# Low parts of tokens and two of four countings on GpSimd, and wider VectorE instructions in the rotation and the counting of an attention and FFN phase

## The chip, the cores and the metric

The kernel runs on one core of a Trainium2 chip. The core has TensorE (PE in the profile; PEld is its weight load), VectorE (DVE), ScalarE (ACT), GpSimd (POOL) and SyncE (SP, which here issues DMAs). The engines run their own instruction streams in order and wait for each other by semaphores. The metric is the device time in microseconds, the median of several runs.

## The reference

Four sequences of 1024 tokens with 256 features pass through two layers. Layer 0 is a gated convolution block with an MLP, and then a mixture of 32 experts. Layer 1 is block-masked attention with rotary positions (16 heads of 16), and then a gated FFN with a 2:4 choice: of every four neighbouring hidden values the two largest in magnitude are kept. What the change touches is in layer 1:

```python
def _rope(x):
    ...
    x1, x2 = jnp.split(x, 2, axis=-1)
    rot = jnp.concatenate([-x2, x1], axis=-1)
    return x * cos + rot * sin
...
def _sparsify_2to4(h):
    g = h.reshape(B, S, I // 4, 4)
    a = jnp.abs(g)
    _, idx = jax.lax.top_k(a, 2)
    pos = jnp.arange(4)
    mask = (pos == idx[..., 0:1]) | (pos == idx[..., 1:2])
    return (g * mask.astype(g.dtype)).reshape(B, S, I)
...
h = jax.nn.silu(jnp.einsum('bsh,hi->bsi', x, w_gate)) * jnp.einsum('bsh,hi->bsi', x, w_up)
h_sparse = _sparsify_2to4(h)
return jnp.einsum('bsi,ih->bsh', h_sparse, w_down)
```

## The kernel before, in words

Three phases run one after the other: `conv_mlp_phase` (layer 0's first half), `experts_phase`, and `attention_ffn_phase` (layer 1), which takes the time from 678 us on. The change lies in the third alone. All tokens stay in `x_sb`, 32 tiles of 128 tokens; a sequence has 8 tiles (`ST`), treated in two halves of 4 (`GT`).

For each sequence `b` the third phase normalises the tokens, projects them to q, k and v, rotates q and k, takes for every head and row of blocks the maximum of the scores, computes the scores again with that maximum subtracted, their exponentials and the weighted sums (`heads`), projects out, normalises, and runs the FFN. FFN of sequence `b` and projections of sequence `c = b + 1` are woven together. I call this stretch a joint; there are three, since the last sequence has nothing after it. In the first it lies at 880 to 1012 us.

The order of each engine is written out by hand, in one function per engine: `@block.sync`, `@block.gpsimd`, `@block.scalar`, `@block.vector`, `@block.tensor`. Within a joint the FFN goes in 16 passes `w`. A pass of PE (`hidden`, L2067) makes 128 hidden features in 24 matmuls, then ACT takes SiLU (`silu`, L1540), DVE multiplies gate and up (`hidden`, L1722: one input in PSUM, one in SBUF; below it is the product of pass `w`), and ACT takes the magnitude (`magnitude`, L1546). PE may be two passes ahead of DVE's product: `hidden(b, w)` on PE waits for `hm_ok` of pass `w - 2`.

The projections of sequence `c` use f16 pairs: a tile is rounded to f16 by ACT (`x_high`, L1478), and what is left is the low part (`x_low`, L1638, on DVE, 256 columns). SP turns both by a transposing DMA (`x_turned`, L1379), which waits for the low part; PE multiplies (`qkv`, L1910) into one bank, ACT copies q and k out of it, then v (`qkv_copied`, L1485, L1488). DVE rotates (`rotate`): q and k times cosine (L1646), times sine (L1649), and two additions (L1652, L1653). ACT makes the high parts and copies (`high_part`, L1495; `part_copies`), DVE the low parts of q and k (`low_parts`, L1658, L1659). In pass `w` DVE does `rotate(c, w + 1)`, the product, `low_parts(c, w + 1)` and `x_low(c, w + 4)`.

The 2:4 choice works on groups of four passes, `k` = 0 to 3: `compare` (L1732 to L1734) compares the magnitudes pairwise into six planes `ge` of bf16, `count` (L1739 to L1747) adds and subtracts these planes to four counts `nb`, and `keep_largest` (L1756, the keep) multiplies the values by whether their count suffices. Three steps share the semaphore `sp`. In a joint, `compare(b, 0)` follows pass 4, `count(b, 0)` pass 5, the keep pass 6; `compare(b, 1)` and `count(b, 1)` follow pass 8, and the second keep comes after two maxima of sequence `c` (L1669) and the product of pass 9. `sparsify(b, 2)` and `sparsify(b, 3)` do the three steps at a stretch. PE's `down` (L2080) needs the kept values.

POOL in this phase computes only the inverse deviations of the layer norms (`inverse_deviation`, L1440 and L1443, on 4 columns) in the order of the list `ORDER`, and sets some columns by memset (`zero_columns`, L1447). The normalisation itself (`normal`, L1622) is DVE's and waits for `rs_ok`.

In the first phase POOL adds and multiplies whole tiles (L234, L239, L247) while DVE convolves (L396, two inputs in SBUF).

Of the kernel before, what the change touches and what calls it, by code (L numbers as in the profile page):

```python
# [22 lines left out]
P = 128  # L23
# [1134 lines left out]
def attention_ffn_phase(nc, io, keep):  # L1158
    with ExitStack() as ctx:  # L1159
# [9 lines left out]
        w_fd = sb("w_fd", [P, NF, D])  # L1169
        cos = sb("cos", [P, ST, HD])  # L1170
        sin = sb("sin", [P, ST, HD])
        mask = sb("mask", [P, 2])
# [5 lines left out]
        qk = sb("qk", [P, 2, 2 * HEADS, HD])  # L1178
        ro = sb("ro", [P, 2 * HEADS, HD])
        sn = sb("sn", [P, 2 * HEADS, HD])  # L1180
        xbT = sb("xbT", [P, KD, SEQ])
# [183 lines left out]
        def _(sync):  # L1365
            for src in ("w_qk", "w_v"):
                sync.dma_start(raw[src].rearrange("p (k c) -> p k c", k=KD), io[src]).then_inc(w_loaded, 16)
            for src, dst in (("mask", mask), ("cos", cos), ("sin", sin)):
                sync.dma_start(dst[:], io[src]).then_inc(consts, 16)
            for src in ("w_fg", "w_fu"):  # L1370
                sync.dma_start(raw[src].rearrange("p (k c) -> p k c", k=KD), io[src]).then_inc(wf_loaded, 16)
            for src, dst in (("w_o", w_o), ("w_fd", w_fd)):
                sync.dma_start(dst[:], io[src]).then_inc(consts, 16)

# [61 lines left out]
        def _(pool):  # L1436
            def inverse_deviation(k):
# [5 lines left out]
                pool.tensor_tensor(rs[:], ve[:], power[:], ALU.pow).then_inc(rs_ok, 1)  # L1443

            def zero_columns(c):
                all_q_max_landed(pool, c)
                pool.memset(all_rows[:, 0, :, NORM:FILTER], 0.0).then_inc(zeroed, 1)  # L1447
# [13 lines left out]
            for k in range(2, len(ORDER)):  # L1461
                kind, b, s = ORDER[k]
                inverse_deviation(k)
                if (kind, s) == ("a", 0) and b + 1 < NB:
                    zero_columns(b + 1)

        @block.scalar
        def _(act):
# [11 lines left out]
            def qkv_copied(c, t):  # L1480
                k = c * ST + t
                wait(act, qkv_mm, k + 1)
                wait(act, turned, 2 * (k - 1))
                bank = tile_bank(c, t)
                act.activation(qk[:, t % 2, :, :].rearrange("p h d -> p (h d)"), bank[:, 0, :], ACT.Copy, scale=1 / W_SCALE)  # L1485
                if t == 0 and c > 0:
                    wait(act, pv_mm, LEAD + c * NHG * NU)
                act.activation(v[:, t, :, 0:HD], bank[:, 1, 0:D].rearrange("p (h d) -> p h d", h=HEADS),  # L1488
                               ACT.Copy, scale=1 / W_SCALE).then_inc(qkv_ok, 1)
# [112 lines left out]
        def _(dve):  # L1602
# [37 lines left out]
            def rotate(c, t):  # L1640
# [4 lines left out]
                wait(dve, low_ok, k)  # L1645
                dve.tensor_tensor(ro[:, :, :], x, cos[:, t, :].unsqueeze(1).to_broadcast([P, 2 * HEADS, HD]),  # L1646
                                  ALU.mult).then_inc(turned, 1)
                wait(dve, rv_ok, k)
                dve.tensor_tensor(sn[:, :, :], x, sin[:, t, :].unsqueeze(1).to_broadcast([P, 2 * HEADS, HD]),  # L1649
                                  ALU.mult).then_inc(turned, 1)  # L1650
                wait(dve, turned, 2 * k + 2)
                dve.tensor_tensor(ro[:, :, 0:HALF_D], ro[:, :, 0:HALF_D], sn[:, :, HALF_D:], ALU.add)  # L1652
# [83 lines left out]
            def count(b, k):  # L1736
                s = 3 * (4 * b + k)
                wait(dve, sp, s + 1)
                dve.tensor_tensor(nb[:, 0, :], ge[:, 0, :], ge[:, 1, :], ALU.add)  # L1739
                dve.tensor_tensor(nb[:, 1, :], ge[:, 3, :], ge[:, 4, :], ALU.add)  # L1740
                dve.tensor_tensor(nb[:, 2, :], ge[:, 1, :], ge[:, 3, :], ALU.add)
                dve.tensor_tensor(nb[:, 3, :], ge[:, 2, :], ge[:, 4, :], ALU.add).then_inc(sp, 1)
                wait(dve, sp, s + 2)
                dve.tensor_tensor(nb[:, 0, :], nb[:, 0, :], ge[:, 2, :], ALU.add)
                dve.tensor_tensor(nb[:, 1, :], nb[:, 1, :], ge[:, 0, :], ALU.subtract)
                dve.tensor_tensor(nb[:, 2, :], nb[:, 2, :], ge[:, 5, :], ALU.subtract)
                dve.tensor_tensor(nb[:, 3, :], nb[:, 3, :], ge[:, 5, :], ALU.add).then_inc(sp, 1)  # L1747

# [31 lines left out]
            def heads(b):  # L1780
                for g in range(NHG):
                    for s in range(STEPS):
# [7 lines left out]
                        if g == NHG - 1:  # L1790
                            if b > 0 and s in (2, 6):
                                finish(b - 1, s // 4)
                            if b + 1 < NB and s in (10, 14):
                                layernorm("x", b + 1, s // 4 - 2)
                if b + 1 < NB:
                    x_low(b + 1, 0)
                    x_low(b + 1, 1)
                normalised(b, NHG - 1, 1)
# [25 lines left out]
            for b in range(NB):  # L1824
# [11 lines left out]
                if ahead:  # L1836
                    x_low(c, 2)
                    rotate(c, 0)
# [4 lines left out]
                normal("a", b, 1)  # L1843
                if ahead:
                    x_low(c, 3)
                for w in range(NF + 1 if ahead else 16):
# [5 lines left out]
                    if ahead and w + 1 < ST:  # L1852
                        low_parts(c, w + 1)
                    if ahead and w + 4 < ST:
                        x_low(c, w + 4)
                    if w >= 4 and w % 4 == 0:
                        compare(b, w // 4 - 1)
                    if w >= 4 and w % 4 == 1 or ahead and w == NF:
                        count(b, w // 4 - 1)
# [369 lines left out]
```

## Time and profile before

| | |
|---|---|
| runs | 1753.49, 1753.75 and 1754.46 us, median 1753.75 |
| profiled execution | 1749.66 us, its span 1747.8 us |
| mean granted clock of TensorE | 0.917 |
| PE busy | 1479.3 us (85%) |
| DVE busy | 1146.7 us (66%) |
| ACT busy | 732.6 us (42%) |
| POOL busy | 219.9 us (13%) |

The profile is of one execution. Busy time of an engine is the time in which at least one of its instructions ran; PE overlaps matmuls, so a busy PE is not a PE at its peak. Two instructions in a row on DVE overlap a little: one of 512 columns lasts 0.68 us and the next starts 0.60 us after it. Such a distance from start to start is what an instruction costs in a row. POOL's 220 us lie almost all in the first two phases.

### The profile page before, as it was taken

To read this page: it belongs to the slowest core of one execution; us is meant where nothing else is said; L and a number is where in the kernel's file an instruction comes from. 1 tells how busy PE (TensorE), PEld (TensorE's weight loads), DVE (VectorE), ACT (ScalarE), POOL (GpSimd) and SP (SyncE) were. 2 spreads that over 40 slices of the span, in tenths; PEclk is the share of its full clock that TensorE was granted. 3 is DMA by queue.
4 is the path that set the end of the run, shared out by engine and by line. 5 is a ranking of instruction groups with operands and counts; after the bars stand their busy time and mean duration, and the time that the engine had idled before them with its cause. 6 is when DMAs were issued, how large, how long until landed. Compare 5 with 4: busy or idle time off the path is not lost.

```text
span 1747.8 us, 25797 instructions
## 1 busy us (share of the span) xinstructions
PE 1479.3 (85%) x9682; PEld 826.3 (47%) x9683; DVE 1146.7 (66%) x2395; ACT 732.6 (42%) x1232; POOL 219.9 (13%) x225
## 2 busy tenths in 40 slices
PE   4999999967989983588878998887998788988796
PEld 2566666653657773223343533253533344433354
DVE  5566666636421135678668769668789578789475
ACT  5454444512212220426744137743147652157530
POOL 3344444411410001000000000100000100000000
PEclk8999999978999987759998979998989898989999
DMA  2000000005105412212101023111013111211000
GB/s 111 13 25 25 24 24 24 28 21 180 40 26 150 149 39 105 47 33 43 31 19 31 1 43 56 40 19 28 17 28 60 38 19 24 37 37 32 31 1 25
DMA packets 137483, 75.21 MB, mean 43 GB/s; under 512 B 117648, under 2 KB 126352, under 8 KB 136592
## 3 DMA queue, kind: packets, MB, share of 16 engines
q1 hardware_dynamic: 136800, 72.02, 16.8%
q0 software_dynamic: 576, 1.77, 0.4%
q8 instruction: 67, 1.10, 0.3%
q14 instruction: 40, 0.33, 0.1%
HBM read 37.59 MB, written 9.06 MB: 27 GB/s over the span
## 4 chain that ended last, share of the span: by engine, by line
issue 59%; POOL 2%; DVE 0%; POOLq 0%; DVEq 0%
POOL rs_sb L1443 1%; POOL ve_sb L1440 0%; POOL qks_sb L1457 0%; POOL v_sb L1455 0%; DVE bn_sb L1607 0%; DVE x_sb_sb L1622 0%; POOLq L1159 0%; POOLq L66 0%; POOL qks_sb L1447 0%; DVE mv_sb L1613 0%; DVEq L1159 0%; POOL v_sb L1454 0%; POOL qks_sb L1458 0%; DVE ident_h_sb L1803 0%; DVEq L66 0%
## 5 line engine op out<-in xcount | busy, mean ns | idle before, releaser
L1509 ACT ACTIVATE room_sb<-s_ps 128x1024 f32<-128x1024 f32 (+1 forms) x320 | 291.2, 941 | 167.1 <-PE s_ps L1965 162.5
L1674 DVE TENSOR_REDUCE mx_sb<-s_ps 128x1 f32<-128x512 f32 (+1 forms) x400 | 249.4, 649 | 63.5 <-PE s_ps L1941 40.2
L1938 PE MATMUL s_ps<-room_sb 48*128 48x512 f16 (+3 forms) x480 | 152.3, 354 | 30.6 <-DVE mx_sb L1669 16.3
L1985 PE MATMUL cm_ps<-room_sb,v_sb 128*32 128x512 f32 (+3 forms) x1536 | 166.2, 522 | 0.8 <-ACT room_sb L1515 0.8
L1965 PE MATMUL s_ps<-room_sb 51*128 51x128 f16 (+4 forms) x1152 | 150.4, 283 | 15.4 <-ACT room_sb L1509 10.6
L2080 PE MATMUL cm_ps<-w_fd_sb,room_sb 128*128 128x256 f32 x512 | 131.6, 405 | 14.6 <-DVE room_sb L1756 14.6
L1440 POOL TENSOR_TENSOR ve_sb<-mv_sb,eps_sb 128x4 f32<-128x4 f32 x24 | 5.0, 210 | 1027.9 <-DVE mv_sb L1613 1027.9
L396 DVE SCALAR_TENSOR_TENSOR x_sb_sb<-xp_sb,conv_w_sb,x_sb_sb 128x512 f32<-128x512 f32 x96 | 106.9, 1117 | 22.6 <-ACT x_sb_sb L319 20.5
L2067 PE MATMUL s_ps<-xbT_sb,w_fg_sb 128*128 128x512 f16 x384 | 107.3, 412 | 14.3 <-DVE ctok_sb L1722 12.7
L1938 PEld LDWEIGHTS s_ps<-room_sb 48*128 48x128 f16 x480 | 42.5, 95 | 161.7 <-DVE mx_sb L1674 85.0
L2080 PEld LDWEIGHTS cm_ps<-w_fd_sb,room_sb 128*128 128x128 f32 x512 | 97.2, 198 | 38.7 <-issue 14.3
L2067 PE MATMUL s_ps<-xbT_sb,w_fu_sb 128*128 128x512 f16 x384 | 102.9, 399 | 0.0
L966 PE MATMUL em_ps<-xT_sb,ws_gu_sb 128*128 128x512 f32 x192 | 92.1, 626 | 8.0 <-DMA rows<-zeros 8.0
L1910 PE MATMUL s_ps<-w_qk_sb,xt_sb 128*128 128x512 f16 x192 | 51.3, 406 | 49.2 <-DMA xt_sb<-xs_sb 31.4
L1965 PEld LDWEIGHTS s_ps<-room_sb 50*128 50x128 f16 (+1 forms) x1152 | 58.5, 97 | 65.8 <-ACT room_sb L1509 44.9
L1941 PE MATMUL s_ps<-room_sb 51*128 51x128 f16 x360 | 69.7, 238 | 19.6 <-DMA room_sb<-qks_sb 12.0
L1674 DVE TENSOR_REDUCE mx_sb<-cm_ps 128x1 f32<-128x512 f32 (+1 forms) x112 | 73.3, 655 | 18.2 <-PE s_ps L1941 13.9
L402 DVE SCALAR_TENSOR_TENSOR m1T_sb<-mm_ps,m1T_sb 128x512 f16<-128x512 f32 x64 | 44.0, 688 | 57.1 <-ACT m1T_sb L311 56.9
L1540 ACT ACTIVATE sgl_sb<-s_ps 128x512 f32<-128x512 f32 x64 | 37.9, 593 | 82.9 <-PE s_ps L2067 82.5
L490 PE MATMUL ro_ps<-w_dn_sb,m1T_sb 128*128 128x256 f16 x256 | 69.8, 273 | 0.8
L491 PE MATMUL ro_ps<-w_dn_sb,m1T_sb 128*128 128x256 f16 x256 | 69.8, 273 | 0.0
L492 PE MATMUL ro_ps<-w_dn_sb,m1T_sb 128*128 128x256 f16 x256 | 69.8, 273 | 0.0
(260 smaller groups left out, 2932.5 us busy)
## 6 DMA issues: line engine op xcount, KB each, us to landing
we_gu_sb<-we_gu SPq DMA_DIRECT2D x32, 352.0 KB
we_dn_sb<-we_dn SPq DMA_DIRECT2D x32, 176.0 KB
x_in_sb<-x SPq DMA_DIRECT2D x9, 512.0 KB, 3.6
rows<-x_sb_sb SPq DMA_DIRECT2D x8, 512.0 KB, 3.0
x_sb_sb<-rows SPq DMA_DIRECT2D x2, 2048.0 KB, 11.4
out<-x_sb_sb SPq DMA_DIRECT2D x8, 512.0 KB, 2.6
room_sb<-qks_sb SPq DMA_TRANSPOSE x88, 3.3
xp_sb<-w_in SPq DMA_DIRECT2D x1, 1024.0 KB, 5.4
```

The source lines that it names most:

```text
L396: dve.scalar_tensor_tensor(xc[:, c, :], xp[:, c, k:k + GTOK], conv_w[:, c, k:k + 1], xc[:, c, :], ALU.mult, ALU.add)\
L490: pe.matmul(out, of[0][at], by[0][cols], start=start, stop=False)
L491: pe.matmul(out, of[1][at], by[0][cols], start=False, stop=False)
L492: return pe.matmul(out, of[0][at], by[1][cols], start=False, stop=stop)
L966: last = pe.matmul(mm[c % 4][:, :], ws_gu[:, k, col:col + P], xT[:, k, g * GTOK:(g + 1) * GTOK], start=(k == 0), stop=(k == KD - 1))
L1509: act.activation(weights[(g * NU + u) % SLOTS_P][:, 2 * pair:2 * pair + 2, 0:width(u) * P], W[s % 2][:, :, 0:width(u) * P], ACT.Exp, scale ...
L1674: dve.tensor_reduce(mx[:, pair, k % 2, slot:slot + 1], max_bank(g, m)[:, 0:count * P], AX.X, ALU.max, negate=True).then_inc(mx_ok, 1)
L1938: last = pe.matmul(bank[:, at * P:(at + plain) * P], query[head:head + NORM, i * P:(i + 1) * P], key[head:head + NORM, j * P:(j + plain) * ...
L1965: last = pe.matmul(W[s % 2][:, head, (at + low - i) * P:(at + high - i) * P], key[first:first + rows, j * P:(j + 1) * P], query[first:firs ...
L1985: last = pe.matmul(O[32 * h:32 * h + 32, (i - half * GT) * P:(i - half * GT + count) * P], v[:, j, g * HG + h, :], weights[(g * NU + u) % ...
L2067: last = pe.matmul(bank[:, e, :], wt[:, j, k, ch * P:(ch + 1) * P], xh[:, g, k, i, :], start=(k == n == 0), stop=(k == KD - 1 and n == 2))
L2080: last = pe.matmul(CM[:, t // 2, (t % 2) * D:(t % 2 + 1) * D], hs[:, k % 3 * 4 + i, t * P:(t + 1) * P], w_fd[:, k % 2 * 4 + i, :], start=( ...
```

## The change

1. `x_low` of the second, third and fourth sequence goes from DVE to POOL (24 instructions; those of the first sequence stay). POOL has them in its list behind the inverse deviations: tiles 0 and 1 behind that of `("x", b, 1)`, tile 2 behind `("a", b, 0)` and ahead of the memset, tiles 3 to 7 behind `("a", b, 1)`.
2. In the three joints `count(b, 0)` and `count(b, 1)` go to POOL, behind tile 7's low part.
3. Counting takes four instructions of two planes each (1024 columns) for eight of one plane, on either engine.
4. `ro` and `sn` become planes of one tile `rosn`, `cos` and `sin` of `tables`, and the two multiplications of a rotation become one instruction of 1024 columns. It has both waits in front, and `turned` counts one step a tile instead of two.

```diff
-        cos = sb("cos", [P, ST, HD])
-        sin = sb("sin", [P, ST, HD])
+        tables = sb("tables", [P, 2, ST, HD])
...
-        ro = sb("ro", [P, 2 * HEADS, HD])
-        sn = sb("sn", [P, 2 * HEADS, HD])
+        rosn = sb("rosn", [P, 2, 2 * HEADS, HD])
+        ro, sn = rosn[:, 0, :, :], rosn[:, 1, :, :]
...
         @block.gpsimd
...
+            def x_low(c, t):
+                k = c * ST + t
+                wait(pool, xs_high, k + 1)
+                xt_landed(pool, k - 2)
+                pool.tensor_tensor(xs[:, t % 2, 1, :], x_tile(c, t), xs[:, t % 2, 0, :], ALU.subtract).then_inc(xs_low, 1)
+
+            def count(b, k):
+                s = 3 * (4 * b + k)
+                wait(pool, sp, s + 1)
+                wait(pool, hs_ok, 4 * b + k)
+                pool.tensor_tensor(nb[:, 0:2, :], ge[:, 0:4:3, :], ge[:, 1:5:3, :], ALU.add)
+                pool.tensor_tensor(nb[:, 2:4, :], ge[:, 1:3, :], ge[:, 3:5, :], ALU.add).then_inc(sp, 1)
+                wait(pool, sp, s + 2)
+                pool.tensor_tensor(nb[:, 0:4:3, :], nb[:, 0:4:3, :], ge[:, 2:6:3, :], ALU.add)
+                pool.tensor_tensor(nb[:, 1:3, :], nb[:, 1:3, :], ge[:, 0:6:5, :], ALU.subtract).then_inc(sp, 1)
...
                 inverse_deviation(k)
-                if (kind, s) == ("a", 0) and b + 1 < NB:
-                    zero_columns(b + 1)
+                if (kind, s) == ("x", 1):
+                    x_low(b, 0)
+                    x_low(b, 1)
+                if kind == "a" and b + 1 < NB:
+                    x_low(b + 1, 2 + s)
+                    if s == 0:
+                        zero_columns(b + 1)
+                    else:
+                        for t in range(4, ST):
+                            x_low(b + 1, t)
+                        for n in range(2):
+                            count(b, n)
...
         @block.vector
...
-                dve.tensor_tensor(ro[:, :, :], x, cos[:, t, :].unsqueeze(1).to_broadcast([P, 2 * HEADS, HD]),
+                wait(dve, rv_ok, k)
+                dve.tensor_tensor(rosn[:, :, :, :], x.unsqueeze(1).to_broadcast([P, 2, 2 * HEADS, HD]),
+                                  tables[:, :, t, :].unsqueeze(2).to_broadcast([P, 2, 2 * HEADS, HD]),
                                   ALU.mult).then_inc(turned, 1)
-                wait(dve, rv_ok, k)
-                dve.tensor_tensor(sn[:, :, :], x, sin[:, t, :].unsqueeze(1).to_broadcast([P, 2 * HEADS, HD]),
-                                  ALU.mult).then_inc(turned, 1)
-                wait(dve, turned, 2 * k + 2)
+                wait(dve, turned, k + 1)
...
-                dve.tensor_tensor(nb[:, 0, :], ge[:, 0, :], ge[:, 1, :], ALU.add)
-                dve.tensor_tensor(nb[:, 1, :], ge[:, 3, :], ge[:, 4, :], ALU.add)
-                dve.tensor_tensor(nb[:, 2, :], ge[:, 1, :], ge[:, 3, :], ALU.add)
-                dve.tensor_tensor(nb[:, 3, :], ge[:, 2, :], ge[:, 4, :], ALU.add).then_inc(sp, 1)
+                dve.tensor_tensor(nb[:, 0:2, :], ge[:, 0:4:3, :], ge[:, 1:5:3, :], ALU.add)
+                dve.tensor_tensor(nb[:, 2:4, :], ge[:, 1:3, :], ge[:, 3:5, :], ALU.add).then_inc(sp, 1)
...
-                if ahead:
-                    x_low(c, 2)
                     rotate(c, 0)
...
-                    if ahead and w + 4 < ST:
-                        x_low(c, w + 4)
...
-                    if w >= 4 and w % 4 == 1 or ahead and w == NF:
+                    if not ahead and w >= 4 and w % 4 == 1:
                         count(b, w // 4 - 1)
```

How the order of the engines changes is shown at two places. The first is POOL in the first joint, from the inverse deviation of the first half of the attention's output on (`xs_sb` holds the f16 pairs, `room_sb` the planes `ge`, `nb_sb` the counts). Before:

```order
L1440 TENSOR_TENSOR ve_sb<-mv_sb,eps_sb 128x4
L1443 TENSOR_TENSOR rs_sb<-ve_sb,power_sb 128x4
L1447 MEMSET qks_sb 128x128x2
L1440 TENSOR_TENSOR ve_sb<-mv_sb,eps_sb 128x4
L1443 TENSOR_TENSOR rs_sb<-ve_sb,power_sb 128x4
```

Now:

```order
L1442 TENSOR_TENSOR rs_sb<-ve_sb,power_sb 128x4
L1448 TENSOR_TENSOR xs_sb<-x_sb_sb,xs_sb 128x256
L1462 MEMSET qks_sb 128x128x2
L1439 TENSOR_TENSOR ve_sb<-mv_sb,eps_sb 128x4
L1442 TENSOR_TENSOR rs_sb<-ve_sb,power_sb 128x4
L1448 TENSOR_TENSOR xs_sb<-x_sb_sb,xs_sb 128x256 x5
L1454 TENSOR_TENSOR nb_sb<-room_sb 128x1024
L1455 TENSOR_TENSOR nb_sb<-room_sb 128x1024
L1457 TENSOR_TENSOR nb_sb<-nb_sb,room_sb 128x2x512
L1458 TENSOR_TENSOR nb_sb<-nb_sb,room_sb 128x1024
```

A low part now stands between the first inverse deviation and the memset, five more behind the second, and then the counts, of which the first is shown; the second follows at once.

The second place is DVE from the second comparison of a joint to the keep behind it. Before:

```order
L1734 TENSOR_TENSOR room_sb<-room_sb 128x512
L1739 TENSOR_TENSOR nb_sb<-room_sb 128x512
L1740 TENSOR_TENSOR nb_sb<-room_sb 128x512
L1741 TENSOR_TENSOR nb_sb<-room_sb 128x512
L1742 TENSOR_TENSOR nb_sb<-room_sb 128x512
L1744 TENSOR_TENSOR nb_sb<-nb_sb,room_sb 128x512
L1745 TENSOR_TENSOR nb_sb<-nb_sb,room_sb 128x512
L1746 TENSOR_TENSOR nb_sb<-nb_sb,room_sb 128x512
L1747 TENSOR_TENSOR nb_sb<-nb_sb,room_sb 128x512
L1669 TENSOR_REDUCE mx_sb<-s_ps 128x2 x2
L1722 SCALAR_TENSOR_TENSOR room_sb<-s_ps,sgl_sb 128x512
L1756 SCALAR_TENSOR_TENSOR room_sb<-nb_sb,ctok_sb 128x512 x4
```

Now:

```order
L1758 TENSOR_TENSOR room_sb<-room_sb 128x512
L1693 TENSOR_REDUCE mx_sb<-s_ps 128x2 x2
L1746 SCALAR_TENSOR_TENSOR room_sb<-s_ps,sgl_sb 128x512
L1776 SCALAR_TENSOR_TENSOR room_sb<-nb_sb,ctok_sb 128x512 x4
L1693 TENSOR_REDUCE mx_sb<-s_ps 128x2 x2
```

The eight counting instructions are gone from between the comparison and the maxima; the keep, two maxima and one product later, waits for POOL's count, and two more maxima stand behind it.

## Rows read from the trace of the kernel before

**Rows 1.** The page, part 1: busy time of each engine (share of the span).

```profile
PE 1479.3 (85%) x9682; PEld 826.3 (47%) x9683; DVE 1146.7 (66%) x2395; ACT 732.6 (42%) x1232; POOL 219.9 (13%) x225
```

**Rows 2.** Waits of PE, 880 to 1012 us: total, times, longest.

```profile
PE s_ps L2067 <- DVE ctok_sb L1722: 4.2, 2, 3.6
...
PE cm_ps L2080 <- DVE room_sb L1756: 3.3, 1, 3.3
...
PE s_ps L1938 <- DVE mx_sb L1669: 2.5, 1, 2.5
```

**Rows 3.** Timeline of DVE, first joint: start, us, instruction [idle before <-releaser].

```profile
908.84 0.42 DVE L1638 TENSOR_TENSOR xs_sb<-x_sb_sb,xs_sb 128x256 f16<-128x256 f32 x1 [1.43 <-ACT xs_sb L1478]
...
914.14 0.42 DVE L1638 TENSOR_TENSOR xs_sb<-x_sb_sb,xs_sb 128x256 f16<-128x256 f32 x1 [1.43 <-ACT xs_sb L1478]
...
932.03 0.68 DVE L1734 TENSOR_TENSOR room_sb<-room_sb 128x512 bf16<-128x512 f32 x1
...
932.63 0.68 DVE L1646 TENSOR_TENSOR ro_sb<-qk_sb,cos_sb 128x512 f32<-128x512 f32 x1
...
936.09 0.42 DVE L1739 TENSOR_TENSOR nb_sb<-room_sb 128x512 bf16<-128x512 bf16 x1
...
938.90 0.68 DVE L1646 TENSOR_TENSOR ro_sb<-qk_sb,cos_sb 128x512 f32<-128x512 f32 x1
...
940.89 0.68 DVE L1722 SCALAR_TENSOR_TENSOR ctok_sb<-s_ps,sgl_sb 128x512 f32<-128x512 f32 x1
```

**Rows 4.** Timeline of PE, same joint.

```profile
936.68 1.46 PE L2067 MATMUL s_ps<-xbT_sb,w_fu_sb 128*128 128x512 f16 x6
...
941.72 2.72 PE L2067 MATMUL s_ps<-xbT_sb,w_fg_sb 128*128 128x512 f16 x6 [3.58 <-DVE ctok_sb L1722]
...
959.02 0.39 PE L1938 MATMUL s_ps<-room_sb 48*128 48x256 f16 x1
...
963.31 12.79 PE L2080 MATMUL cm_ps<-w_fd_sb,room_sb 128*128 128x256 f32 x58
```

**Rows 5.** Timeline of DVE, around the second comparison and keep.

```profile
951.08 0.68 DVE L1734 TENSOR_TENSOR room_sb<-room_sb 128x512 bf16<-128x512 f32 x1
...
955.87 2.49 DVE L1756 SCALAR_TENSOR_TENSOR room_sb<-nb_sb,ctok_sb 128x512 f32<-128x512 bf16 x4
```

**Rows 6.** Groups of POOL by line: count | busy us, mean ns | idle before.

```profile
L247 POOL TENSOR_TENSOR yT_sb<-x_sb_sb,yT_sb 128x512 f16<-128x512 f32 x32 | 35.9, 1153 | 0.0
...
L731 POOL TENSOR_TENSOR su_sb<-sg_sb,su_sb 128x512 f32<-128x512 f32 x9 | 11.4, 1262 | 47.3 <-ACT su_sb L767 47.3
...
L736 POOL TENSOR_TENSOR x_sb_sb<-x_sb_sb,so_sb 128x1024 f32<-128x1024 f32 x8 | 18.8, 2351 | 137.7 <-ACT so_sb L773 137.7
```

**Rows 7.** L396 (ns min/median/max), then timelines of DVE and POOL, first phase.

```profile
L396 DVE SCALAR_TENSOR_TENSOR x_sb_sb<-xp_sb,conv_w_sb,x_sb_sb x96: 734/752/2760, 19.7 to 325.5; 128x512 f32<-128x512 f32 x96
...
98.23 2.75 DVE L396 SCALAR_TENSOR_TENSOR x_sb_sb<-xp_sb,conv_w_sb,x_sb_sb 128x512 f32<-128x512 f32 x1
...
97.88 2.56 POOL L234 TENSOR_TENSOR x_sb_sb<-x_in_sb,x_sb_sb 128x1024 f32<-128x1024 f32 x1
...
102.94 1.68 POOL L239 TENSOR_TENSOR x_sb_sb<-x_sb_sb 128x512 f32<-128x512 f32 x1 [2.50 <-ACT x_sb_sb L296]
```

**Rows 8.** Timelines of DVE and POOL, start of the third phase.

```profile
686.53 5.72 DVE L1622 TENSOR_SCALAR x_sb_sb<-x_sb_sb,mv_sb,rs_sb 128x256 f32<-128x256 f32 x3 [1.49 <-POOL rs_sb L1443]
...
688.22 2.91 POOL L1457 MEMSET qks_sb<- 128x1664 f16 x2
```

**Rows 9.** Group of DVE by line, 1024 f32.

```profile
L1773 DVE TENSOR_TENSOR x_sb_sb<-cm_ps,x_sb_sb 128x1024 f32<-128x1024 f32 x8 | 9.7, 1217 | 2.5 <-PE cm_ps L2080 2.5
```

**Rows 10.** Timeline of ACT, same joint.

```profile
913.43 0.37 ACT L1488 ACTIVATE v_sb<-s_ps 128x256 f32<-128x256 f32 x1
```

**Rows 11.** DMA issues, 895 to 935 us: count, median us to landing.

```profile
xt_sb<-xs_sb SPq DMA_TRANSPOSE x6, 2.5
```

**Rows 12.** Stretches: us, busy of PE, PEld, DVE, ACT, POOL, PEclk, DMA, GB/s.

```profile
955.00:961.20 6.20, 6.11 (x21) 1.78 (x21) 5.11 (x10) 1.23 (x2) 0.00 (x0) 0.50 0.00 0
```

More of the change, by code:

```diff
@@ L1367, in _ @@
                 sync.dma_start(raw[src].rearrange("p (k c) -> p k c", k=KD), io[src]).then_inc(w_loaded, 16)
-            for src, dst in (("mask", mask), ("cos", cos), ("sin", sin)):
-                sync.dma_start(dst[:], io[src]).then_inc(consts, 16)
+            for src, dst in (("mask", mask), ("cos", tables[:, 0, :, :]), ("sin", tables[:, 1, :, :])):
+                sync.dma_start(dst if src in ("cos", "sin") else dst[:], io[src]).then_inc(consts, 16)
             for src in ("w_fg", "w_fu"):
@@ L1372, in _ @@
             for src, dst in (("w_o", w_o), ("w_fd", w_fd)):
-                sync.dma_start(dst[:], io[src]).then_inc(consts, 16)
+                sync.dma_start(dst if src in ("cos", "sin") else dst[:], io[src]).then_inc(consts, 16)
             def x_turned(c, t):
@@ L1482, in qkv_copied @@
                 wait(act, qkv_mm, k + 1)
-                wait(act, turned, 2 * (k - 1))
+                wait(act, turned, k - 1)
                 bank = tile_bank(c, t)
@@ L1738, in count @@
                 wait(dve, sp, s + 1)
-                dve.tensor_tensor(nb[:, 0, :], ge[:, 0, :], ge[:, 1, :], ALU.add)
-                dve.tensor_tensor(nb[:, 1, :], ge[:, 3, :], ge[:, 4, :], ALU.add)
-                dve.tensor_tensor(nb[:, 2, :], ge[:, 1, :], ge[:, 3, :], ALU.add)
-                dve.tensor_tensor(nb[:, 3, :], ge[:, 2, :], ge[:, 4, :], ALU.add).then_inc(sp, 1)
+                dve.tensor_tensor(nb[:, 0:2, :], ge[:, 0:4:3, :], ge[:, 1:5:3, :], ALU.add)
+                dve.tensor_tensor(nb[:, 2:4, :], ge[:, 1:3, :], ge[:, 3:5, :], ALU.add).then_inc(sp, 1)
                 wait(dve, sp, s + 2)
[L1744 to L1747, printed above, removed]
+                dve.tensor_tensor(nb[:, 0:4:3, :], nb[:, 0:4:3, :], ge[:, 2:6:3, :], ALU.add)
+                dve.tensor_tensor(nb[:, 1:3, :], nb[:, 1:3, :], ge[:, 0:6:5, :], ALU.subtract).then_inc(sp, 1)
             def keep_largest(b, k):
@@ L1794, in heads @@
                                 layernorm("x", b + 1, s // 4 - 2)
-                if b + 1 < NB:
-                    x_low(b + 1, 0)
-                    x_low(b + 1, 1)
                 normalised(b, NHG - 1, 1)
@@ L1843, in _ @@
                 normal("a", b, 1)
-                if ahead:
-                    x_low(c, 3)
                 for w in range(NF + 1 if ahead else 16):
```

## The prediction

> **What bounds the kernel now.** I read the busy times first: TensorE (PE) works 85% of the span, VectorE (DVE) 66%, GpSimd (POOL) 13% [rows 1]. PE's waits in the first joint (880 to 1012 us, where the FFN of one sequence meets the projections of the next) come next: 4.2 us for the gated products L1722, 2.5 us for a maximum, 3.3 us for kept values L1756 [rows 2]. All three are DVE's. There are three such joints (sequences 0 to 1, 1 to 2, 2 to 3), and only there does the change move work to POOL. DVE's timeline shows why it is late: after the first comparison ends, at 932.63, it still has to rotate, count and rotate again before the product of pass 6 at 940.89, for which PE sat idle 3.58 us [rows 3, 4]. After the second comparison it counts until the keep at 955.87, and PE stalls again [rows 4, 5]. So DVE's order sets the end here; work that leaves DVE is worth something only if nothing in that order then waits for POOL.
>
> **What POOL charges.** A two-input instruction of 512 f32 takes 1.262 us there and of 1024 f32 2.351, so 2.13 ns an element and 0.17 fixed; with f16 in one input and the output, 512 take 1.153 [rows 6]. A counting instruction has 1024 elements, all bf16, a form that no row has. From above the 1024 f32 row bounds it: 2.35. From below I let 16 bits halve the element part, as they do on DVE (0.42 for 512 bf16 against 0.68 in f32 [rows 3]): 1.26. I take twice 1.153 less one fixed part, 2.13, since the f16 row is the nearest. A count is 4 of these, 8.6 us with its inner wait (4.9 to 9.5), against 2.8 us on DVE (936.09 to 938.90) [rows 3]. A low part (256) is half the 512 f16 row less the fixed part's share: about 0.6.
> The page GPSIMD Engine Reference of the Trainium skill (3.1, side-by-side cycle accounting) gives 4497 ns for 2048 f32 elements; 1024 would be an estimated 2.25 us, a count 9.0, and the predicted time 3 us higher (0.12 for each of 8 instructions in 3 joints). The row of 1024 f32 here is 4% above that figure; the page says nothing of 16 bits, and the f16 row is 9% under its f32 fellow.
>
> **What POOL does to DVE.** This decides the case. In the first phase a DVE instruction with both inputs in SBUF (L396, median 0.752 us) that starts beside a 2.56 us POOL instruction lasts 2.75 and ends 0.54 after it; the other way round a POOL instruction of 512 f32, 1.262 alone, becomes 1.68 while DVE finishes [rows 6, 7]. So they take turns, whole instructions at a time. The normalisation L1622 is worse off: three of them, 768 elements and so less work than the 1.217 us of 1024, need 5.72 us beside a row of memsets on POOL, and do not get in between these [rows 8, 9]. In the joint, rotations, low parts of q and k, and keeps all have two SBUF inputs. Maxima and gated products read PSUM and at most one tile of SBUF.
> SBUF — State Buffer of the Trainium skill (Who interferes with whom) makes this a rule against the change: a DVE instruction with two SBUF inputs contends with a POOL instruction that reads SBUF. The rows show it for f32; for bf16 no run here does yet.
>
> **The change part by part**, for one joint, against the trace.
> (a) Low parts. Off DVE they save 0.34 each (0.42 less what overlaps), plus the wait for ScalarE: period of a pass 908.84 to 914.14 is 5.30, of which 1.43 waits [rows 3]. The next rotation then starts when q and k are copied (913.43 and 0.37 [rows 10]) instead of 0.68 later. But POOL's low part becomes ready 0.3 after that, during the multiplication, and goes before the additions, which wait 0.55 to 0.6: DVE gives back most of it. With the fused multiplication (next) a pass gains 0.3; four passes, -1.2. The other four stand in POOL's queue in front of or among normalisations: two before the normalisation of x (+0.3, since 0.7 of their DVE time also goes), one with the memset before that of the first half (+0.8 - 0.34), one before the second (+0.6 - 0.34). Each low part also releases the transposing DMA of its tile; it now ends some 1.7 us into a pass, and 2.5 us later [rows 11] the tile has landed, still before the 5.0 at which PE's next projection finds its bank free: no cost. What else stands behind POOL's new work, the inverse deviations, is asked for only 8 us or more later.
> (b) Fused rotation. Two multiplications of 512 are issued 0.60 apart; an instruction of 1024 f32 lasts 1.217 [rows 9] and lets the next start some 0.08 sooner, 1.13. That is -0.07 a rotation, -0.14 for the two outside the passes. (a) and (b): -1.2 + 0.3 + 0.46 + 0.26 - 0.14 = -0.3. The bounds are -3.4 (no turns lost) and +1.
> (c) First count. Let C be the end of the first comparison. Before: product of pass 6 ends at C+8.9, second comparison ends C+19.05 (951.08 + 0.60) [rows 3, 5]. After: multiplication to C+1.15, then in turns POOL 2.0 (a queued one is issued early), addition 0.3, POOL 2.0, addition, product 5 beside POOL's third, low part, POOL's fourth to C+10.1. Then low part, rotation 7 (2.0) and product 6 end at C+12.9, keep C+13.7 to 16.1, product 7 C+16.8. PE starts its pass 8 at C+12.95 rather than C+9.1 and needs twice 1.46 less their overlap, 2.6 us, or 5.2 at the lower clock [rows 4]; the second comparison ends at C+20.8 or C+22.7. I take the middle: +2.7. With the low price it is +0.3, with the high one +3.6.
> (d) Second count. Nothing contends here, but the keep waits for all of it: from the comparison's end, E, it began at E+4.2 (955.87 - 951.68) [rows 5]; now at E+0.1+8.4 = E+8.5, +4.3. Queued behind it on DVE are the maxima that PE needs for 959.02 [rows 4], so PE moves by the same. Two maxima and a product in front of it run earlier, which helps nobody past it. PE then idles some 8 us. After the 2.5 us idle for a maximum the granted clock was 0.50 (1.2 GHz) [rows 2, 12], and after the 3.58 us six matmuls took 2.72 us instead of 1.46 [rows 4]; so the rest of pass 11 (4.29 us [rows 4], half of it at full clock) goes slowly: +1.2 (-0.8 to +2). Together +5.5; low price +1.2, high +7.
> (e) The other counts stay on DVE: 4 instructions of 0.34 + 0.27 instead of 8 of 0.34 is 2.4 for 2.7, -0.3. The third is hidden behind PE's down products (from 963.31 [rows 4]); the fourth is what L2080 waits for [rows 2], so -0.3 per joint.
> Sum: -0.3 + 2.7 + 5.5 - 0.3 = +7.6 a joint, +22.8 for three. The last sequence has its counts on DVE, -0.9 for the three that are not hidden, and the first rotations give -0.3: **+21.6**. The profiled execution (span 1747.8 in 1749.66) becomes 1771.3; the median of the runs is 1753.75, 4.1 above it, so the predicted time is 1775.
>
> **The rivals.** First, DVE isn't held by 16-bit counts and half-f16 low parts: place, the two rotations after C. For it: no row shows such a pair. Against it: every f32 pair of the first phase takes turns. Then (a) and (b) give -3.4 and (c) gives -1.0 at 2.13 but -2.8 once a count is under 6.5 us; (d) stays. At the middle price that is -3.4 - 1.0 + 5.5 - 0.3 = +0.8, or 1755; at 1.26 it is -5.3 a joint, 17 in all: 1737. It turns faster below some 2.0 us an instruction.
> Second, turns are taken but bf16 runs at the low price: -0.3 + 0.3 + 1.2 - 0.3 = +0.9 a joint, less 1.2: 1755, hardly to be told from no change.
> Third, the high price, PE slow for all of pass 8 and pass 11 and no gain from (a): +1 + 5.5 + 7 - 0.3 = +13 a joint, 1792. For it speaks that PE's longest idle here, 3.58 us, already halved the clock, and that (d) makes one of 8.
>
> **How the numbers follow.** Forecast 0.62 (1775); not held 0.08; cheap bf16 0.12; dear and slow 0.18. A run of this kernel can be told from no change at 0.2%, 3.5 us. Faster by more than that needs the first rival at a low price: 0.08. Within it lies most of the second: 0.10. Slower: 0.82. The range 1755 to 1794 leaves out the first rival, half of the second and little of the third. Its ends are the bounds of the counting instruction's price.
>
> **What would show it.** In the new profile: POOL's counting instructions at 2.0 to 2.2 us; the rotation right after the first comparison drawn out over some 9 us; the second keep about 8.5 us behind its comparison with DVE idle for POOL; a wait of PE for a maximum of some 8 us, followed by a 0.50 clock; POOL's low parts beside lengthened additions. I am wrong if the counting rows are near 1.2 us, if rotations beside them keep their usual durations, or if PE's total wait in a joint shrinks.

## The result, and the profile after

The changed kernel takes 1779.6 us (median of four runs, 1779.17 to 1781.71) against 1753.62 for the kernel before beside it: 1.0156 times as long, 95% interval 1.0136 to 1.0176. 1775 was predicted, in a range of 1755 to 1794, so the slowdown is 26 us for 21.6. The profiled execution has a span of 1777.8 us at a mean granted clock of 0.907.

The first line of the page answers to [rows 1]: VectorE's busy time hardly moves, GpSimd gains 80 us, and TensorE is busy 10 us longer with the same matmuls.

```profile
PE 1489.0 (84%) x9682; PEld 834.3 (47%) x9683; DVE 1145.8 (64%) x2251; ACT 733.4 (41%) x1232; POOL 299.7 (17%) x273
```

TensorE's waits in the first joint (880 to 1022 us; total, times, longest) answer to [rows 2]:

```profile
PE s_ps L1950 <- DVE mx_sb L1693: 9.1, 1, 9.1
PE s_ps L2079 <- DVE ctok_sb L1746: 6.6, 2, 4.2
...
PE cm_ps L2092 <- DVE room_sb L1776: 3.1, 1, 3.1
```

The wait for a maximum (2.5 before) is 9.1 us and the one for products (4.2) is 6.6. VectorE's timeline of that joint (L1672 is the fused multiplication, L1676 and L1677 the additions, L1746 the product, L1682 and L1683 the low parts of q and k, L1758 the end of a comparison, L1776 the keep):

```profile
909.99 1.23 DVE L1672 TENSOR_TENSOR rosn_sb<-qk_sb,tables_sb 128x1024 f32<-128x1024 f32 x1 [1.12 <-ACT v_sb L1513]
911.25 0.78 DVE L1676 TENSOR_TENSOR rosn_sb<-rosn_sb 128x256 f32<-128x256 f32 x1
...
914.94 1.23 DVE L1672 TENSOR_TENSOR rosn_sb<-qk_sb,tables_sb 128x1024 f32<-128x1024 f32 x1 [1.13 <-ACT v_sb L1513]
...
932.68 1.22 DVE L1672 TENSOR_TENSOR rosn_sb<-qk_sb,tables_sb 128x1024 f32<-128x1024 f32 x1
933.93 2.22 DVE L1676 TENSOR_TENSOR rosn_sb<-rosn_sb 128x256 f32<-128x256 f32 x1
936.08 2.33 DVE L1677 TENSOR_TENSOR rosn_sb<-rosn_sb 128x256 f32<-128x256 f32 x1
938.33 0.68 DVE L1746 SCALAR_TENSOR_TENSOR ctok_sb<-s_ps,sgl_sb 128x512 f32<-128x512 f32 x1
939.10 1.57 DVE L1682 TENSOR_TENSOR qks_sb<-rosn_sb,qks_sb 128x256 f16<-128x256 f32 x1
940.60 2.34 DVE L1683 TENSOR_TENSOR qks_sb<-rosn_sb,qks_sb 128x256 f16<-128x256 f32 x1
...
945.08 0.68 DVE L1746 SCALAR_TENSOR_TENSOR ctok_sb<-s_ps,sgl_sb 128x512 f32<-128x512 f32 x1
...
946.53 2.49 DVE L1776 SCALAR_TENSOR_TENSOR room_sb<-nb_sb,room_sb 128x512 f32<-128x512 bf16 x4
...
954.42 0.68 DVE L1758 TENSOR_TENSOR room_sb<-room_sb 128x512 bf16<-128x512 f32 x1
...
963.68 2.50 DVE L1776 SCALAR_TENSOR_TENSOR room_sb<-nb_sb,ctok_sb 128x512 f32<-128x512 bf16 x4 [7.31 <-POOL nb_sb L1458]
```

GpSimd's timeline, the two counts (first and last instruction of each; beside the first one the durations include turns with VectorE):

```profile
932.84 3.03 POOL L1454 TENSOR_TENSOR nb_sb<-room_sb 128x1024 bf16<-128x1024 bf16 x1 [5.56 <-DVE room_sb L1758]
...
940.35 2.31 POOL L1458 TENSOR_TENSOR nb_sb<-nb_sb,room_sb 128x1024 bf16<-128x1024 bf16 x1
955.18 2.13 POOL L1454 TENSOR_TENSOR nb_sb<-room_sb 128x1024 bf16<-128x1024 bf16 x1 [12.52 <-DVE room_sb L1758]
...
961.53 2.11 POOL L1458 TENSOR_TENSOR nb_sb<-nb_sb,room_sb 128x1024 bf16<-128x1024 bf16 x1
```

Beside the first count the two additions and the two low parts, 0.42 us each otherwise, take 2.22, 2.33, 1.57 and 2.34: 6.8 us more together, while the product between them keeps its 0.68. The same four are drawn out in the other two joints, to within 0.01 us. The count's result is not late: it ends at 942.66, and the first keep comes only at 946.53. Nothing is stretched beside the second count, but the keep stands idle for it. TensorE's timeline, and below it the stretches (us, busy times, PEclk the granted clock):

```profile
939.06 2.39 PE L2079 MATMUL s_ps<-xbT_sb,w_fg_sb 128*128 128x512 f16 x6 [4.19 <-DVE ctok_sb L1746]
...
945.91 2.38 PE L2079 MATMUL s_ps<-xbT_sb,w_fg_sb 128*128 128x512 f16 x6 [2.39 <-DVE ctok_sb L1746]
948.08 2.27 PE L2079 MATMUL s_ps<-xbT_sb,w_fu_sb 128*128 128x512 f16 x6
950.18 1.46 PE L2079 MATMUL s_ps<-xbT_sb,w_fg_sb 128*128 128x512 f16 x6
...
966.83 0.39 PE L1950 MATMUL s_ps<-room_sb 48*128 48x256 f16 x1 [9.10 <-DVE mx_sb L1693]
```

```profile
966.80:972.70 5.90, 5.87 (x17) 1.37 (x17) 2.84 (x5) 0.92 (x2) 0.00 (x0) 0.50 0.00 0
972.70:987.50 14.80, 14.80 (x60) 12.45 (x58) 9.73 (x13) 0.94 (x2) 0.00 (x0) 0.85 0.01 2
...
1147.00:1156.30 9.30, 8.09 (x30) 6.80 (x29) 1.23 (x1) 1.33 (x2) 0.00 (x0) 0.60 0.02 4
```

After the 9.1 us of idling the rest of pass 11 runs wholly at 1.2 GHz (0.50), and the first 60 down matmuls need 14.8 us at 0.85. In the other two joints pass 11 is slow as well, but the down matmuls run at 1.00 and 0.99. (The last line belongs to the entry of the second joint, below.)

Where the time goes, from one mark of the two profiles to the next (after less before, us):

| stretch of a joint | predicted | first | second | third |
|---|---|---|---|---|
| attention residual (L1788) to C, end of the first comparison | -0.3 | -1.1 | -1.4 | -1.4 |
| C to E, end of the second comparison | +2.7 | +3.3 | +5.5 | +3.1 |
| E to the second keep | +4.3 | +4.5 | +4.5 | +4.5 |
| second keep to the first residual (L1793) | +1.2 | +3.7 | +0.4 | +1.7 |
| first to second residual | -0.3 | -1.3 | -1.5 | +1.3 |
| second residual to the next joint's L1788 | 0 | +2.8 | +2.2 | -1.0 |

That is 25.7 inside the joints and 4.0 between them, with 1.2 ahead of the first joint and -1.0 in the last sequence: 30 us between the two profiled executions, where the medians differ by 26. The 4.0 are of one pair of executions, and the one of before was 4.1 us under its own median. The low parts need not be behind them. With none of them on GpSimd the last stretch of the table takes 122.3 us behind the first joint in one run below (fused rotation and two planes alone) and 122.3 behind the second in another (low parts back on VectorE); it is 119.3 and 120.1 before, 122.1 and 122.3 now. At the entry of the second joint the order is the same in both but for the low parts, and TensorE's output projection had a clock of 0.79 before (next line) and 0.60 after (last line above):

```profile
1135.00:1143.30 8.30, 7.08 (x33) 6.29 (x34) 1.23 (x1) 1.33 (x2) 0.00 (x0) 0.79 0.16 32
```

### The profile page after: what moved, and what is told of

It reads as the page before. It is cut to its first block and busy times, and to the rows that moved or that the text cites. A ratio compares the mean times of both kernels' runs of the same rounds, so it can differ in the third digit from the quotient of the medians.

```text
span 1777.8 us, 25737 instructions
## 1 busy us (share of the span) xinstructions
PE 1489.0 (84%) x9682; PEld 834.3 (47%) x9683; DVE 1145.8 (64%) x2251; ACT 733.4 (41%) x1232; POOL 299.7 (17%) x273
## 5 line engine op out<-in xcount | busy, mean ns | idle before, releaser
L2079 PE MATMUL s_ps<-xbT_sb,w_fg_sb 128*128 128x512 f16 x384 | 108.8, 417 | 20.8 <-DVE ctok_sb L1746 19.4
L396 DVE SCALAR_TENSOR_TENSOR x_sb_sb<-xp_sb,conv_w_sb,x_sb_sb 128x512 f32<-128x512 f32 x96 | 106.8, 1115 | 22.6 <-ACT x_sb_sb L319 20.5
```

What stands on the lines that cost most here:

```text
L396: dve.scalar_tensor_tensor(xc[:, c, :], xp[:, c, k:k + GTOK], conv_w[:, c, k:k + 1], xc[:, c, :], ALU.mult, ALU.add)\
L2079: last = pe.matmul(bank[:, e, :], wt[:, j, k, ch * P:(ch + 1) * P], xh[:, g, k, i, :], start=(k == n == 0), stop=(k == KD - 1 and n == 2))
```

## The experiments

My theory: the second count costs by its latency, since the keep waits for it with maxima queued behind, and by the clock after that; the first costs by turns with two-input instructions on VectorE; the other parts gain a little. The first four kernels take the change apart.

**Both counts back on VectorE**

```diff
-                        for n in range(2):
-                            count(b, n)
...
-                    if not ahead and w >= 4 and w % 4 == 1:
+                    if w >= 4 and w % 4 == 1 or ahead and w == NF:
                         count(b, w // 4 - 1)
```

> Edit: the changed kernel with the first and second count of every joint back on VectorE (in two planes); low parts of tokens stay on GpSimd, the fused rotation stays. Theory (the second count makes the keep wait for GpSimd and TensorE drops its clock; the first count takes turns with rotations; the other parts gain a little): the first count cost about 10 to 12 us (the end of the second comparison moved by 3.3, 5.5 and 3.1 us in the three joints), the second about 19 (three times 4.5 and some 6 of clock), so 1748.5 us, 1745 to 1752, a little below the kernel before at 1753.6. Rival A (the low parts on GpSimd, in front of normalisations and beside rotations, are what costs): it stays above 1765. Rival B (the fused rotation or the two-plane counts are slower than what they replace): above 1756.

Measured: 1746.3 us, 0.9958 of before (0.9940 to 0.9975), as the theory has it; rivals A and B fall. The rest of the change is a small gain, and the counts on GpSimd cost more than the whole slowdown, 33 us by the medians. TensorE still waits for maxima behind the count and the keep (first joint):

```profile
PE s_ps L1948 <- DVE mx_sb L1691: 4.0, 2, 2.6
```

**Only the first count, and only the second, on GpSimd**

```diff
-                        for n in range(2):
-                            count(b, n)
+                        count(b, 0)
```

(and `count(b, 1)` in the other; VectorE does the one that is left.)

> Edit: the changed kernel with the second count of every joint back on VectorE; only the first one is on GpSimd. Theory (second count costs more than the first): 1748.5 and the 10 to 12 us of the first count, 1759 us, 1755 to 1763; GpSimd's counting instructions and the rotation beside them still end one after the other, the second keep no longer waits. Rival C (the turns are the main cost, the wait of the keep is covered by other work): 1770 to 1777. Rival A (the low parts cost): above 1770 as well, but then also without any count on GpSimd.

> Edit: the changed kernel with the first count of every joint back on VectorE; only the second one is on GpSimd. Theory: 1748.5 and the 19 us of the second count, 1767 us, 1762 to 1772; the second keep begins about 8.6 us behind its comparison and TensorE waits some 8 us for a maximum. Rival C (turns are the main cost): 1750 to 1757.

Measured: 1760.0 us (1.0034, 1.0017 to 1.0050) and 1761.3 us (1.0039, 1.0023 to 1.0054). So the first count costs 13.8 us and the second 15.1 over the kernel without them. Between the marks, against that kernel, the first keep comes 4.55 later in the joint with the first count on GpSimd, and the second keep 4.7 later with the second: three times each is 13.7 and 14.2. The second by itself is just under the range given. Each moved count costs about the same, where the theory had 10 to 12 us for the first and 19 for the second; rival C falls too. Both together, the changed kernel, are 0.0198 of 1754 or 35 us over the kernel with neither: some 6 more than the sum, which is about what the intervals leave open. In the profiles the part of it that can be seen is the clock: from the second keep to the first residual the kernel with both takes 2.6, 0.4 and 0.6 us longer than the one with the second count alone, and in the first joint TensorE's first 60 down matmuls behind that keep take 12.7 us at full clock with the second count alone, and 14.8 at 0.85 with both.

**Low parts of tokens back on VectorE**

```diff
-                    x_low(b + 1, 2 + s)
...
-                        for t in range(4, ST):
-                            x_low(b + 1, t)
...
+                    if ahead and w + 4 < ST:
+                        x_low(c, w + 4)
```

> Edit: the changed kernel with all low parts of tokens back on VectorE where they were; both counts stay on GpSimd. Theory (the low parts on GpSimd gain 1.1 to 1.4 us a joint, of which up to 0.3 is the fused rotation): 3 to 4 us slower than the changed kernel's 1779.6, 1783 us, 1780 to 1786. Rival A (the low parts cost): 1760 to 1772. Rival D (they neither gain nor cost): within 1 us of 1779.6.

Measured: 1781.3 us, 1.0156 of before (1.0143 to 1.0169), the same ratio as the changed kernel, so rival D by the ratios, although the median itself lies in the theory's range: the run does not decide between them. The profile does show the gain in the passes: a period of 5.24 here against 4.95 in the changed kernel (909.99 to 914.94 above), with the wait for ScalarE's high part (1.43) back in place of that for its copy (1.13 there):

```profile
913.01 0.43 DVE L1657 TENSOR_TENSOR xs_sb<-x_sb_sb,xs_sb 128x256 f16<-128x256 f32 x1 [1.43 <-ACT xs_sb L1497]
...
918.25 0.43 DVE L1657 TENSOR_TENSOR xs_sb<-x_sb_sb,xs_sb 128x256 f16<-128x256 f32 x1 [1.43 <-ACT xs_sb L1497]
```

From the attention residual to C the move gains 1.06, 1.04 and 0.96 us in the three joints (44.96 against 43.90 in the first). Together that is 3.1 us, less than the intervals are wide.

**Fused rotation and two planes alone**

The edit joins the two before: no count and no low part on GpSimd.

> Edit: the kernel with only the fused rotation and the counts in two planes; low parts of tokens and all counts are on VectorE, GpSimd gets nothing new. With counts on VectorE and low parts on GpSimd the time was 1746.3 us. Theory (as measured on the changed kernel, moving the low parts changes the time by no more than 1.5 us): 1747 us, 1745 to 1749.5, so the gain over the kernel before comes from the fused rotation and the two planes. Rival (the low parts on GpSimd gain once no count stands behind them): 1750 to 1754.

Measured: 1747.4 us, 0.9968 (0.9954 to 0.9981). These two edits make the gain, 5.6 us. What the low parts add (0.9958 against 0.9968) stays inside the intervals, so their worth to the whole kernel is not settled.

**The keep moved behind the maxima**

If the second count costs by what is queued behind its keep, one moved line must give it back.

```diff
                         hidden(b, w - 1)
-                        if w == 10:
-                            keep_largest(b, 1)
                         maxima(c, 0, m + 2, m + 4)
                     hidden(b, 11)
+                    keep_largest(b, 1)
                     sparsify(b, 2)
```

> Edit: the changed kernel with one line moved: the second keep of a joint stands after the maxima and the products of passes 10 and 11, right before the third comparison; the count that it needs is still on GpSimd. Theory (the second count costs by what is queued behind the waiting keep, and by the clock after it): the 4.7 us a joint and the clock behind it go, and the 2.6 and 1.3 us that TensorE waits for a maximum behind count and keep go too: 1760 us with the first count's price left, less up to 12: 1750 us, 1746 to 1762; TensorE's wait of some 9 us for a maximum is under 1 us. Rival E (what GpSimd does during that time slows VectorE's maxima and products as well, or the keep's wait moves on to the down products): 1768 to 1780.

Measured: 1742.4 us, 0.9930 (0.9909 to 0.9952): 37 us less than the changed kernel, with both counts still on GpSimd, and 3.6 below the range. TensorE's waits of the first joint have no row for a maximum any more. The price of the second count is gone and more with it. Against the kernel with the first count alone, the end of the second comparison to the first residual takes 6.5, 5.9 and 6.1 us less, and I had allowed for the 3.9 of the two waits. The rest is the clock: pass 11 and the down products now run at full clock (stretches of this run; compare 0.50 and 0.85 above), while with the first count alone the end of pass 11 had 0.50 in the first joint:

```profile
957.90:963.90 6.00, 6.00 (x35) 1.96 (x33) 4.82 (x10) 2.50 (x5) 5.75 (x3) 1.00 0.00 0
963.90:976.60 12.70, 12.70 (x60) 10.93 (x58) 10.96 (x16) 1.06 (x2) 2.65 (x2) 1.00 0.01 2
```

**The same with the first count on VectorE, and with all counts there**

```diff
-                        for n in range(2):
-                            count(b, n)
+                        count(b, 1)
```

(the keep late as above; in the second kernel neither count is on GpSimd, and `count(b, 1)` stands ahead of the late keep on VectorE.)

> Edit: as the run before it (second keep late), and the first count back on VectorE; second count on GpSimd. Theory: 1746.3 us of both counts on VectorE, less the waits of TensorE for a maximum behind the second count and keep (2.6 and 1.3 us a joint): 1736 us, 1733 to 1743; GpSimd's counting instructions 2.1 us each, since maxima and products read PSUM. Rival E: 1750 to 1765.

> Edit: no count on GpSimd; on VectorE the second count and the second keep both stand late, right before the third comparison. Theory (the place in VectorE's order decides, not the engine that counts): the maxima come as early as with the count on GpSimd, and the later count and keep of 4.9 us are still done before the second half of the down products needs them: 1736 us, 1733 to 1744, within 2 us of the run with the count on GpSimd. Rival F (it pays only because GpSimd does the counting, the late count delays the down products): 1744 to 1752.

Measured: 1729.5 us, 0.9866 (0.9846 to 0.9885), for the first, which beats both kernels, by 24 and by 50 us, and lies 3.5 us below the range. Again it is the clock that I had left out: in the first joint the kernel with both counts on VectorE ran the end of pass 11 at 0.50 and this one at 1.00. Its VectorE and GpSimd beside each other in the first joint:

```profile
950.21 0.69 DVE L1692 TENSOR_REDUCE mx_sb<-s_ps 128x2 f32<-128x512 f32 x1
...
957.62 2.50 DVE L1775 SCALAR_TENSOR_TENSOR room_sb<-nb_sb,ctok_sb 128x512 f32<-128x512 bf16 x4 [1.31 <-POOL nb_sb L1458]
```

```profile
949.11 2.12 POOL L1454 TENSOR_TENSOR nb_sb<-room_sb 128x1024 bf16<-128x1024 bf16 x1 [23.20 <-DVE room_sb L1757]
...
955.46 2.13 POOL L1458 TENSOR_TENSOR nb_sb<-nb_sb,room_sb 128x1024 bf16<-128x1024 bf16 x1
```

Maxima and products, which read PSUM, keep their durations beside the count (0.69 and 0.68), and the count keeps its 2.12.

With all counts on VectorE it is 1738.9 us, 0.9922 (0.9897 to 0.9947): by the ratios the place in VectorE's order alone gives 6 of the 16 us (0.0036 and 0.0092 of 1754) that lie between both counts on VectorE and the second one on GpSimd with a late keep. Rival F falls, but that the engine wouldn't matter was wrong: 1738.9 is 9 us above the run with the count on GpSimd, not within 2. The count ahead of the late keep puts the third comparison 1.2 us later, TensorE then waits 1.1 us for a maximum at the end of the first down products, and in the second and third joint its clock falls. These stretches of the second joint, of the run with all counts on VectorE and of the one with the second on GpSimd, both go from the first residual to the end of the fourth comparison:

```profile
1216.80:1240.60 23.80, 23.80 (x100) 9.92 (x99) 17.27 (x28) 4.75 (x8) 0.00 (x0) 0.90 0.00 1
```

```profile
1221.40:1243.00 21.60, 21.60 (x100) 9.95 (x100) 17.22 (x29) 4.75 (x8) 0.00 (x0) 1.00 0.00 1
```

The same hundred matmuls take 2.2 us longer.

**What holds VectorE beside the first count**

Starting from the kernel with both counts on VectorE, GpSimd gets idle work at the place of the first count, for which nobody waits.

```diff
+            def beside_first(b):
+                wait(pool, sp, 12 * b + 1)
+                other = w_fg[:, 0, :, :].rearrange("p k c -> p (k c)").bitcast(BF16)
+                for i in range(4):
+                    pool.wait_ge(setup, 3 + 4 * b + i)
+                    pool.tensor_tensor(spare[:, 0:2, :], other[:, 0:1024].rearrange("p (k c) -> p k c", k=2),
+                                       other[:, 1024:2048].rearrange("p (k c) -> p k c", k=2), ALU.add).then_inc(setup, 1)
```

(or six times `pool.memset(spare[:, :, :], 0.0)`.)

> Edit: from the run with both counts on VectorE (1746.3 us) GpSimd gets four additions of 1024 bf16 elements more in each joint, from when the first comparison ends, over weights that don't change into a tile that nobody reads; the real counts stay on VectorE. So no one waits for their results, and what they cost is contention alone. Theory (GpSimd's 16-bit additions and VectorE's instructions with two inputs in SBUF take turns): each addition holds VectorE about as the first count did, 4.5 us of TensorE's time a joint and up to 2.4 more since VectorE has its own count to do beside them: 1760 to 1767 us; instructions of rotation, count and low parts after the first comparison are drawn out by 1 to 2 us each. Rival G (the first count cost because its result came late): 1745 to 1749, VectorE's durations unchanged.

> Edit: the same with six memsets of 1536 bf16 elements on GpSimd in place of the four additions, about as long together (8 to 9 us). They read nothing. If any SBUF access of GpSimd holds VectorE (the memsets on the page of before held a normalisation for 5.7 us): 1758 to 1767, as with the additions. If only reading ones do: 1745 to 1749, and VectorE's instructions after the first comparison keep their durations. The theory leaves this open; I expect the second, with rotations and counts unchanged, at 6 in 10.

Measured: 1770.7 us with the additions (1.0094, 1.0063 to 1.0125), 24 over the kernel without them and 4 above the range, into which its interval reaches; 1748.2 with the memsets (0.9961, 0.9944 to 0.9977), within its noise. VectorE and then GpSimd beside the additions:

```profile
930.98 1.21 DVE L1680 TENSOR_TENSOR rosn_sb<-qk_sb,tables_sb 128x1024 f32<-128x1024 f32 x1
932.22 2.23 DVE L1684 TENSOR_TENSOR rosn_sb<-rosn_sb 128x256 f32<-128x256 f32 x1
934.37 2.33 DVE L1685 TENSOR_TENSOR rosn_sb<-rosn_sb 128x256 f32<-128x256 f32 x1
...
937.40 1.57 DVE L1690 TENSOR_TENSOR qks_sb<-rosn_sb,qks_sb 128x256 f16<-128x256 f32 x1
938.89 2.34 DVE L1691 TENSOR_TENSOR qks_sb<-rosn_sb,qks_sb 128x256 f16<-128x256 f32 x1
```

```profile
931.13 9.82 POOL L1466 TENSOR_TENSOR spare_sb<-w_fg_sb 128x1024 bf16<-128x1024 bf16 x4 [5.56 <-DVE room_sb L1766]
```

And beside the memsets:

```profile
933.66 1.22 DVE L1678 TENSOR_TENSOR rosn_sb<-qk_sb,tables_sb 128x1024 f32<-128x1024 f32 x1
934.91 0.42 DVE L1682 TENSOR_TENSOR rosn_sb<-rosn_sb 128x256 f32<-128x256 f32 x1
935.26 0.42 DVE L1683 TENSOR_TENSOR rosn_sb<-rosn_sb 128x256 f32<-128x256 f32 x1
```

```profile
933.80 8.56 POOL L1465 MEMSET spare_sb<- 128x1536 bf16 x6 [5.54 <-DVE room_sb L1764]
```

The four stretched instructions are to 0.01 us those of the changed kernel, 6.8 us together, and the first keep comes 6.79 later than without the additions. So the first count's cost is contention, not a late result, and rival G falls. Where GpSimd counts, VectorE is spared its own count, 2.5 us from start to start, of which 0.3 goes in a gap ahead of the next rotation: less that, the 6.79 are the 4.55 which the first count cost.

## Why the prediction was right

**Direction and place** held: both counts cost where they were said to, one by turns on VectorE and one by a keep that waits. Of the rows named as signs, the second keep idles 7.31 us and comes at E+8.66 for a predicted E+8.5 (955.02 to 963.68), and the wait for a maximum is 9.1 us with a clock of 0.50 behind it. One sign was put too high: the rotation right after the first comparison lasts 5.7 us (932.68 to 938.41), not some 9; with the low parts of q and k behind it, it is 10.3.

**The price of a counting instruction**, the unknown on which the range rested, was taken as 2.13 us between 1.26 and 2.35; it is 2.11 to 2.13 in the second count, where nothing contends. Sixteen bits gain GpSimd little (2.351 for 1024 f32 [rows 6]). The second rival, cheap bf16, falls by this row, the first, no turns, by the stretched additions. Of the third the high price falls by the same row, but the slow clock that it had in passes 8 and 11 is for the most part there in the first joint. The range's upper end was not, as the prediction says, the bound of this price: with 2.35 its own terms give -0.3 + 3.6 + 7 - 0.3 = +10 a joint, some 1782, and 1794 lies just above the third rival. The measured 1779.6 is inside either. The GPSIMD Engine Reference of the Trainium skill (3.1) gave an estimated 2.25 by its f32 figure; the measured 2.12 is 6% under that.

**(c), the first count.** The steps came out in the first joint: product of pass 6 ends at C+13.1 (C+12.9 predicted), keep at C+13.85 (C+13.7). The mis-sized step is "I take the middle" between the two clocks of pass 8: TensorE ran it mostly at the lower one, its two groups of six matmuls in 2.38 and 2.27 us (a pass has 12 matmuls, not the 24 given where the kernel is described), and the comparison ended at C+22.4 for a predicted C+20.8 or C+22.7. That is +3.3 instead of +2.7, and +3.1 in the third joint. The +5.5 of the second has two halves that no term foresaw: the kernel before took only 17.99 us from C to E there (19.05 in the first), and the changed one took 23.53 (22.35).

**(d), the second count.** The +4.3 of waiting are 4.5. The clock's +1.2 were taken for pass 11 alone, where the first joint has +1.6 (966.83 to 972.7 for 4.29); what the step left out is the down products behind it, which there also ran slow (12.79 us for 58 before [rows 4], 14.8 for 60). From the keep to the first residual it is +3.7, +0.4 and +1.7, a mean of 1.9.

**(a) and (b)** gained 1.1 to 1.4 us before C instead of 0.3. The pass is as predicted (4.95 us for 5.0), though the additions give back 0.36 (0.78 for 0.42) instead of 0.55 to 0.6. What failed is the 1.0 us for the entry (0.3 + 0.46 + 0.26): from the residual to the first rotation only 0.2 to 0.3 were lost.

**(e)** held in size: each of the later counts is 0.27 shorter. That the last sequence is 1.0 shorter (0.9 predicted) is partly luck: 0.4 of it lie before its first comparison, where nothing was changed, and its counts give 0.5.

**The total** owes something to errors that cancel. Over three joints (c) was 3.8 short and (d) 2.7 with its wait; (a) and (b) gained 3.0 more than predicted, and the stretch between the residuals 0.6 more. That leaves 2.9 of the 8.4 us by which the sum is short of the two profiled executions (21.6 for 30.0); the other 5.5 lie ahead of the first joint and between the joints. No run here ties those between the joints to the change: behind the first joint the kernels of the experiments need 118.6 to 122.8 us for the stretch to the next one. By the medians the sum is only 4.4 short.

On the SBUF — State Buffer page of the Trainium skill (Who interferes with whom) a VectorE instruction with two SBUF inputs contends with a GpSimd instruction that reads SBUF, and not with one that only writes. Both halves hold here in 16 bits: 2.23 for 0.42 us beside the additions, 0.42 beside the memsets.

## What to carry to other kernels

Before moving a step to a slower engine, look at what its consumer has queued behind it: here one moved line, the keep behind the maxima, was worth 37 us, more than the change had cost. Then count the instructions with two SBUF inputs that VectorE runs meanwhile, for each can wait for a whole GpSimd instruction (2.2 to 2.3 us for 0.42 here), and put GpSimd's reading work beside instructions that read PSUM, as the fastest run here does. A stall of TensorE can cost more than its length: behind the 9.1 us wait in the first joint pass 11 and the down products ran at a lower clock and took 3.7 us more than before.

## What the runs showed of the hardware that was not expected

GpSimd's additions and VectorE's instructions with two SBUF inputs alternated one for one: in every joint a queue of four 2.1 us instructions stretched exactly four instructions on VectorE, of 0.42 us each when alone. The multiplication of 1.2 us that was already running kept its length, and it was GpSimd's first instruction that became longer (3.03 us). Six memsets in their place, 8.6 us together, stretched nothing there, though memsets had held the normalisation, a form with one large input, so that three took 5.72 us [rows 8]. And a wait of TensorE of only 1.1 us at the end of the first down products had a stretch at 0.90 behind it in the second joint and at 0.91 in the third, where the same wait in the first was followed by one at 1.00; what made the difference stays open.
